# Attention in a graph network: both heads of a pair turned in one run of five pieces, two pairs behind the scores

## The chip, the core and the metric

The kernel runs on one core of a Trainium2 chip. The metric is device time in microseconds (us) from start to end of one launch, the median of several runs. Engines: TensorE (PE, with weight loads as PEld), VectorE (DVE), ScalarE (ACT), GpSimd (POOL) and the sync engine (SP), which issues DMAs.

## What is computed

A graph network over 1250 nodes with 512 features: a two-layer graph attention block, then a transformer block of two layers. The change touches only the attention of the transformer's layers, which is this part of the reference (cut):

```python
for l in range(L):                                   # L = 2, H = 8 heads of DH = 64
    q = ((x @ Wq[l].T + bq[l]) * scaling).reshape(n, H, DH)
    k = (x @ Wk[l].T).reshape(n, H, DH)
    v = (x @ Wv[l].T).reshape(n, H, DH)
    scores = jnp.einsum('ehd,ehd->eh', q[tgt], k[srcidx])
    m = jax.ops.segment_max(scores, tgt, num_segments=n)
    p = jnp.exp(scores - m[tgt])
    s = jax.ops.segment_sum(p, tgt, num_segments=n)
    w = p / (s[tgt] + 1e-16)
    agg = jax.ops.segment_sum(w[:, :, None] * v[srcidx], tgt, num_segments=n)
    attn = agg.reshape(n, D) @ Wo[l].T + bo[l]
    ...
```

The kernel does it densely: each score row of 1250 gets the logarithm of the edge count added (a large negative number where there is no edge), so a plain softmax over all nodes is the softmax over the edges.

## The kernel before

Nodes come in T = 10 tiles of P = 125 rows, heads in pairs (head 2c and 2c + 1 share 128 partitions of q and k). A unit u is one head of one tile of target nodes; a pair p is units 2p and 2p + 1; there are 80 units and 40 pairs in each of the two layers. `attend_parts` writes one program for each engine, all unrolled, and they meet in semaphores only.

**PE** (line 2017): for each p it makes the scores of pair p into banks 0 to 4 of PSUM (`score`, L1982, 18 matmuls of three precision passes), transposes the ten blocks of the even unit of pair p - 1 (`turn`, L2000), multiplies the turned probabilities of pair p - 2 with v (`weigh`, L2009, 40 matmuls, two heads side by side), and transposes the ten blocks of the odd unit of pair p - 1. A unit's transposes come in three pieces of 4, 3 and 3 blocks (`CUTS`). The pieces and the result of `weigh` (`out_bank`) take turns in banks 5, 6 and 7 (`ring`), seven tenants per pair. A piece may be written when the bank's former tenant is copied out.

**VectorE** (line 2106): for each p `mask` of both units (L2087: scores plus logs, and the row's maximum, in one instruction out of PSUM), now and then `lower_w` (L2104: low halves of a weight of the next stage), then for each of the two units `safe` (L2092), the reciprocal (L2096) and `divide` (L2098), which follow the unit's exponential.

**ScalarE** (line 2059): copies of the turned pieces to `probs_t` (`save_turned`, L2042), the exponential of the even unit (L2034), the copy of the result of pair p - 2 (`save_att`, L2049), the exponential of the odd unit, the copies of the odd unit's pieces, now and then `cut_w` (L2057).

`probs` has four slots, one per unit, `probs_t` four. The next score may start when both masks of the pair before are done, since it writes the same banks (`pe.wait_ge(masked, 2 * p)`). The weighing waits for the copies of its own pair and for the first copy of the run that precedes it, which empties its bank. The sync engine loads log tiles and weights in step with `masked` and `scored`. Before `attend` each layer projects q, k and v; after it comes a stage of its own (`stage_tail`).

Of the kernel before, what the change touches and what calls it, by code (L numbers as in the profile page):

```python
# [16 lines left out]
BANK = 512  # L17
# [1404 lines left out]
class LayerBuffers:  # L1422


    def __init__(self, k, ctx, gat, base, hidden):
# [21 lines left out]
        self.probs = self.wq  # L1447
        self.in_high = base
        ctx.enter_context(nc.sbuf_tensor("layer_room", [128, (self.e + 8 * D - base) // 4], F32))

# [397 lines left out]
def attend_parts(k, ctx, places, q_chunks, k_high, k_low, v_rows, logs, log_rows, weights, sources, att, x_rows, ln_b, x_biased):  # L1848
# [13 lines left out]
    TENANTS = 2 * PIECES + 1  # L1862
    biased = k.layer == 0
# [7 lines left out]
    probs_t = at("probs_t", [P, TURNED, T, P], F32, places.probs + 4 * SLOTS * N)  # L1871
    neg_max, sums, sums_safe, inverse = (sb(what, [P, COLUMNS]) for what in ("neg_max", "sums", "sums_safe", "inverse"))
# [7 lines left out]
    for rows, high, low in weights:  # L1880
# [4 lines left out]
    cut_at.update({(CHUNKS - 1) * PER_CHUNK + 3 + i: len(cuts) - late + i for i in range(late)})  # L1885
    shared_done, scored, masked, exp_done, sum_safe, inverted, divided, piece_turned, piece_saved, summed, att_saved = (
        k.sem(f"{what}_att{k.layer}") for what in ("shared_done", "scored", "masked", "exp_done", "sum_safe", "inverted", "divided",
                                          "piece_turned", "piece_saved", "summed", "att_saved"))

# [9 lines left out]

    def ring(pair, tenant):  # L1900
        return (5 + (pair * TENANTS + tenant) % 3) * BANK

    def turned(u, j):
        lo, hi = CUTS[j]
        at = ring(u // 2, j if u % 2 == 0 else PIECES + 1 + j)
        return k.psum[0:P, at:at + (hi - lo) * P]

    def out_bank(p):
        at = ring(p + 1, PIECES)
        return k.psum[:, at:at + P]  # L1910

# [3 lines left out]
    def own(odd):  # L1915
        return slice(odd * CH, (odd + 1) * CH)

    def column(u):
        return slice(u % COLUMNS, u % COLUMNS + 1)

    def attend_sync(sp):
# [42 lines left out]
    def attend_tensor(pe, by_rows):  # L1964
# [22 lines left out]

        def turn(u):
            q, odd = u // 2, u % 2
            pe.wait_ge(divided, u + 1)  # L1990
            for j, (lo, hi) in enumerate(CUTS):
                if odd and j == PIECES - 1:
                    if q >= 1:
                        pe.wait_ge(att_saved, q)
                elif odd:
                    pe.wait_ge(piece_saved, 2 * q * PIECES + j + 2)
                elif q >= 1:
                    pe.wait_ge(piece_saved, (2 * q - 1) * PIECES + j + 1)
                for i in range(lo, hi):
                    block_t = pe.transpose(turned(u, j)[:, (i - lo) * P:(i - lo + 1) * P],  # L2000
                                           probs[:, u % SLOTS, i * P:(i + 1) * P], k.ident[0:P, 0:P])
                block_t.then_inc(piece_turned, 1)

        def weigh(p):
            pe.wait_ge(piece_saved, (2 * p + 2) * PIECES + (1 if p + 1 < PAIRS else 0))
            for i in range(T):
                for u in (2 * p, 2 * p + 1):
                    odd, h = u % 2, u % H
                    total = pe.matmul(out_bank(p)[own(odd)], v_rows[:, i, h * CH:(h + 1) * CH],  # L2009
                                      probs_t[:, u % TURNED, i], start=i == 0, stop=i == T - 1)  # L2010
            total.then_inc(summed, 1)
# [4 lines left out]
        pe.wait_ge(k.q_low_done, CHUNKS)  # L2016
        for p in range(PAIRS + 2):
            if p < PAIRS:
                score(p)
            if p == 0:  # L2020
                by_rows(CHUNKS - 1, (1,))
            if p == 1:
                pe.wait_ge(k.v_saved, CHUNKS + 1)
            if 1 <= p <= PAIRS:
                turn(2 * p - 2)
            if p >= 2:
                weigh(p - 2)
            if 1 <= p <= PAIRS:
                turn(2 * p - 1)

    def attend_scalar(act, save_last_v):
        def exponential(u):
            act.wait_ge(masked, u + 1)
            act.activation(probs[:, u % SLOTS], probs[:, u % SLOTS], ACT.Exp, scale=-1.0,  # L2034
                           bias=neg_max[:, column(u)], accum_out=sums[:, column(u)]).then_inc(exp_done, 1)

        def save_turned(u):
            if u >= TURNED:
                act.wait_ge(summed, (u - TURNED) // 2 + 1)
            for j, (lo, hi) in enumerate(CUTS):  # L2040
                act.wait_ge(piece_turned, u * PIECES + j + 1)
                act.copy(probs_t[:, u % TURNED, lo:hi].rearrange("p c n -> p (c n)"), turned(u, j)).then_inc(piece_saved, 1)  # L2042

        def save_att(p):
            t = tile_of(2 * p)
            if p == 0:
                act.wait_ge(k.cols_stored, 16)
            act.wait_ge(summed, p + 1)
            act.copy(att[:, p % PER_TILE, t * P:(t + 1) * P], out_bank(p)).then_inc(att_saved, 1)  # L2049
# [9 lines left out]
        for p in range(PAIRS + 2):  # L2059
            if 1 <= p <= PAIRS:  # L2060
                save_turned(2 * p - 2)
# [6 lines left out]
            if p >= 2:  # L2068
                save_att(p - 2)
            if p < PAIRS:  # L2070
                exponential(2 * p + 1)
            if 1 <= p <= PAIRS:
                save_turned(2 * p - 1)
            if p in cut_at:
                cut_w(cut_at[p])

    def attend_vector(dve):
        def mask(u):
# [6 lines left out]
            if u >= SLOTS:  # L2085
                dve.wait_ge(piece_turned, (u - SLOTS + 1) * PIECES)
# [3 lines left out]
        def safe(u):  # L2090
            dve.wait_ge(exp_done, u + 1)
            dve.tensor_scalar(sums_safe[:, column(u)], sums[:, column(u)], TINY, None, ALU.add).then_inc(sum_safe, 1)  # L2092

        def divide(u):
            dve.wait_ge(sum_safe, u + 1)
            dve.reciprocal(inverse[:, column(u)], sums_safe[:, column(u)]).then_inc(inverted, 1)  # L2096
            dve.wait_ge(inverted, u + 1)
            dve.tensor_scalar(probs[:, u % SLOTS], probs[:, u % SLOTS], inverse[:, column(u)], None, ALU.mult  # L2098
                              ).then_inc(divided, 1)
# [5 lines left out]

        for p in range(PAIRS):
            mask(2 * p)
            mask(2 * p + 1)
# [677 lines left out]
```

## Time and profile before

| | us |
|---|---|
| median of 3 runs | 1716.58 (1715.73 to 1717.91) |
| the profiled execution | 1712.33 |
| its span | 1710.5 |
| PE busy in the span | 1554.0 (91%) |
| VectorE busy | 1293.1 (76%) |
| ScalarE busy | 1168.1 (68%) |

The mean granted clock of PE is 0.965 of full speed. The attention of layer 0 lies from about 876 to 1160 us of the span, that of layer 1 from about 1317 to 1601. The chain of work that ended last covers only the final stage, so it says nothing of these stretches; they are read from windows and from the timeline of a pair. A "releaser" is what ended an engine's idle time before an instruction.

### The profile page before, as it was taken

The numbers are of one execution on the slowest core, as the hardware profiler recorded it, in microseconds if no ns is written. First come the engines' busy times: TensorE is split into PE (matmuls) and PEld (weight loads), VectorE is DVE, ScalarE is ACT, GpSimd is POOL, SyncE is SP. The second block draws the span as 40 slices with busy tenths as digits, with TensorE's granted clock in tenths as the row PEclk, the third lists the DMA queues.
The fourth block names the chain that finished last, engine by engine and source line by source line (L and its number), as shares of the span: only waits on it lengthen the run. The fifth ranks groups of instructions, "written<-read, shape, count | busy, mean of one in ns | idle before, by whom it ended". The sixth has DMA issues, their size and how long they took to land. (4 is left out here: it accounts for less than half of the span.)

```text
span 1710.5 us, 35777 instructions
## 1 busy us (share of the span) xinstructions
PE 1554.0 (91%) x14602; PEld 1418.9 (83%) x14602; DVE 1293.1 (76%) x2259; ACT 1168.1 (68%) x2171; POOL 54.5 (3%) x67
## 2 busy tenths in 40 slices
PE   6899899999995888798999999998799999999882
PEld 3787899999975777787988888888798889889882
DVE  6995999989468999995347777776722777777577
ACT  3454788888655999896457788783433878888434
POOL 0000000000000100000000000001100000000030
PEclk9999899999997999899999999999899999999995
DMA  5113222300006321112412211104110021000401
GB/s 183 55 54 99 84 71 89 111 31 2 1 1 177 120 93 62 61 32 75 123 63 62 60 53 29 35 5 135 49 72 1 19 65 30 17 14 2 116 13 60
DMA packets 58517, 103.53 MB, mean 61 GB/s; under 512 B 15569, under 2 KB 33713, under 8 KB 58352
## 3 DMA queue, kind: packets, MB, share of 16 engines
q1 hardware_dynamic: 58352, 101.22, 19.0%
q8 instruction: 117, 1.92, 0.5%
q14 instruction: 48, 0.39, 0.1%
HBM read 75.74 MB, written 19.21 MB: 56 GB/s over the span
## 5 line engine op out<-in xcount | busy, mean ns | idle before, releaser
L2042 ACT COPY probs_t_att<-banks 125x375 f32<-125x375 f32 (+1 forms) x480 | 211.1, 515 | 73.9 <-PE banks L2000 73.6
L1028 PE MATMUL banks<-ident,probs_gat 125*125 125x125 f32 x1600 | 213.7, 283 | 45.8 <-ACT probs_gat L1132 44.9
L2087 DVE CUSTOM_DVE_ANT_0 probs_att<-banks,logs_or_y 125x1250 f32<-125x1250 f32 x160 | 227.1, 1457 | 28.8 <-PE banks L1982 28.8
L1028 PEld LDWEIGHTS banks<-ident,probs_gat 125*125 125x125 f32 x1600 | 194.5, 195 | 56.3 <-ACT probs_gat L1132 56.0
L1132 ACT ACTIVATE probs_gat<-probs_gat,neg_max_gat 125x1250 f32<-125x1250 f32 x160 | 214.8, 1342 | 33.3 <-DVE neg_max_gat L1301 33.0
L1301 DVE CUSTOM_DVE_ANT_0 probs_gat<-probs_gat,log_counts 125x1250 f32<-125x1250 f32 x160 | 235.3, 1471 | 0.1
L2034 ACT ACTIVATE probs_att<-probs_att,neg_max_att 125x1250 f32<-125x1250 f32 x160 | 216.0, 1350 | 10.0 <-DVE neg_max_att L2087 9.8
L2000 PE MATMUL banks<-ident,probs_att 125*125 125x125 f32 x1600 | 216.5, 282 | 2.9 <-ACT probs_t_att L2042 2.9
L2000 PEld LDWEIGHTS banks<-ident,probs_att 125*125 125x125 f32 x1600 | 186.5, 188 | 30.2 <-issue 16.1
L2009 PE MATMUL banks<-probs_t_att,v_rows 125*64 125x125 f32 x3200 | 189.5, 272 | 6.9 <-ACT probs_t_att L2042 2.0
L2009 PEld LDWEIGHTS banks<-probs_t_att,v_rows 125*64 125x64 f32 x3200 | 170.6, 136 | 22.0 <-ACT probs_t_att L2042 22.0
L1039 PE MATMUL banks<-h,probs_t_gat 125*125 125x128 f32 x1600 | 188.0, 273 | 0.0
L1039 PEld LDWEIGHTS banks<-h,probs_t_gat 125*125 125x125 f32 x1600 | 181.1, 188 | 0.0
L1982 PE MATMUL banks<-k_high,q_chunk 64*125 64x226 f32 (+2 forms) x960 | 158.8, 366 | 4.5 <-DVE q_chunk L1764 2.6
L2098 DVE TENSOR_SCALAR probs_att<-probs_att,inverse_att 125x1250 f32<-125x1250 f32 x160 | 139.5, 872 | 5.6
L1143 ACT COPY probs_t_gat<-banks 125x1250 f32<-125x1250 f32 x120 | 142.9, 1191 | 1.0 <-PE banks L1028 0.7
L1982 PEld LDWEIGHTS banks<-k_high,q_chunk 64*125 64x125 f32 x960 | 126.0, 183 | 15.4 <-issue 3.4
L1295 DVE SCALAR_TENSOR_TENSOR probs_gat<-a_pair,a_dst_gap 125x1250 f32<-125x1250 f32 x80 | 121.1, 1515 | 20.6 <-PE banks L1028 11.0
L1982 PE MATMUL banks<-k_low,q_chunk 64*125 64x512 f32 (+1 forms) x480 | 131.0, 350 | 0.0
L1295 DVE SCALAR_TENSOR_TENSOR probs_gat<-a_pair,a_dst_gap_gat 125x1250 f32<-125x1250 f32 x80 | 121.4, 1519 | 8.9 <-DMA a_pair<-a_src_rows 5.2
L2092 DVE TENSOR_SCALAR sums_safe_att<-sums_att 125x1 f32<-125x1 f32 x160 | 24.5, 153 | 85.8 <-ACT probs_att L2034 84.8
L547 PEld LDWEIGHTS banks<-offset_hot,key_hot_fr 125*125 125x125 bf16 x650 | 73.2, 139 | 16.5 <-DVE offset_hot L361 6.7
(258 smaller groups left out, 2932.4 us busy)
## 6 DMA issues: line engine op xcount, KB each, us to landing
a_pair<-a_src_rows SPq DMA_DIRECT2D x46, 625.0 KB, 4.9
logs_or_y<-log_rows SPq DMA_DIRECT2D x20, 546.9 KB
w_rows<-in_L_gnn_W_dram SPq DMA_DIRECT2D x12, 512.0 KB, 6.5
log_counts<-counts_fr SPq DMA_DIRECT2D x50, 122.1 KB
x_cols<-feature_cols SPq DMA_DIRECT2D x2, 2500.0 KB
logs_or_y<-x_cols SPq DMA_DIRECT2D x10, 500.0 KB, 5.2
x_rows_sb<-in_x_dram SPq DMA_DIRECT2D x1, 2240.0 KB
x_rows<-x_rows_sb SPq DMA_DIRECT2D x10, 224.0 KB
```

The lines of the kernel that those rows point to most:

```text
L1028: block_t = pe.transpose(turned(u)[:, i // 2, (i % 2) * P:(i % 2 + 1) * P], probs[:, u % PROBS, i * P:(i + 1) * P], k.ident[0:P, 0:P])
L1039: total = pe.matmul(out_bank(u), probs_t_slot(u)[:, i], rows, start=i == 0, stop=i == T - 1)
L1132: act.activation(probs[:, u % PROBS], probs[:, u % PROBS], ACT.Exp, scale=-1.0, bias=neg_max[:, column(u)], accum_out=sums[:, column(u)]). ...
L1143: act.copy(probs_t_slot(u).rearrange("p (b c) n -> p b (c n)", c=2), turned(u)).then_inc(probs_saved, 1)
L1295: dve.scalar_tensor_tensor(probs[:, u % PROBS], gat.pair[0:P, head % 2, 0], (gat.gap1, gap2)[layer][:, t, head:head + 1], gat.pair[0:P, he ...
L1301: dve.tensor_tensor_reduce(probs[:, u % PROBS], probs[:, u % PROBS], k.log_counts[:, t], -1.0, -FLOOR, ALU.add, ALU.min, neg_max[:, column ...
L1982: total = pe.matmul(k.psum[0:P, a:b], halves[own(o), half], keys[own(o), c, a - o * N:b - o * N], start=i == 0, stop=i == 2)
L2000: block_t = pe.transpose(turned(u, j)[:, (i - lo) * P:(i - lo + 1) * P], probs[:, u % SLOTS, i * P:(i + 1) * P], k.ident[0:P, 0:P])
L2009: total = pe.matmul(out_bank(p)[own(odd)], v_rows[:, i, h * CH:(h + 1) * CH], probs_t[:, u % TURNED, i], start=i == 0, stop=i == T - 1)
L2034: act.activation(probs[:, u % SLOTS], probs[:, u % SLOTS], ACT.Exp, scale=-1.0, bias=neg_max[:, column(u)], accum_out=sums[:, column(u)]). ...
L2042: act.copy(probs_t[:, u % TURNED, lo:hi].rearrange("p c n -> p (c n)"), turned(u, j)).then_inc(piece_saved, 1)
L2087: dve.tensor_tensor_reduce(probs[:, u % SLOTS], scores(u % 2), logs[:, t % KEPT], -1.0, -FLOOR, ALU.add, ALU.min, neg_max[:, column(u)]).t ...
```

## The change

PE now goes `score(p)`, then all twenty transposes of pair p - 2 in one run (`turn(p - 2)`), then `weigh(p - 3)`. The twenty blocks are five pieces of four, which take banks 5, 6, 7, 5, 6; the result of `weigh` always takes bank 7. So piece 3 waits for the copy of piece 0 and piece 4 for that of piece 1, in the same run; piece 1 of the next pair waits for the copy of piece 4, piece 2 for the copy of the result. `weigh` waits for the first three copies of the run before it.

ScalarE copies four pieces of each pair, then does both exponentials, then the copy of the result. VectorE copies the fifth piece (`save_last`), after the masks; its sum correction and reciprocal do both heads in one instruction each, and they and the divisions belong to pair p - 1. There are six slots of `probs` instead of four, and `probs_t` starts behind them. The room of the layer's buffers grows to hold it. The program is built with a scratch of 4096 bytes for software DMA.

```diff
-    SLOTS = 4
-    TURNED = 4
-    CUTS = ((0, 4), (4, 7), (7, 10))
-    PIECES = len(CUTS)
+    SLOTS, TURNED = places.SLOTS, places.TURNED
+    STEP = 4
+    PIECES = 2 * T // STEP
+    SAVED = PIECES - 1
...
+    def turned(j):
+        at = (5 + j % 3) * BANK
+        return k.psum[0:P, at:at + STEP * P]
...
+    def out_bank():
+        return k.psum[:, 7 * BANK:7 * BANK + P]
...
+        def turn(p):
+            pe.wait_ge(divided, 2 * p + 1)
+            for j in range(PIECES):
+                if j == 0 and p >= 1:
+                    pe.wait_ge(piece_saved, SAVED * p)
+                if j == 1 and p >= 1:
+                    pe.wait_ge(last_saved, p)
+                if j == 2 and p >= 2:
+                    pe.wait_ge(att_saved, p - 1)
+                if j >= 3:
+                    pe.wait_ge(piece_saved, SAVED * p + j - 2)
+                for n in range(j * STEP, (j + 1) * STEP):
+                    u, i = 2 * p + n // T, n % T
+                    if n == T:
+                        pe.wait_ge(divided, 2 * p + 2)
...
         def weigh(p):
-            pe.wait_ge(piece_saved, (2 * p + 2) * PIECES + (1 if p + 1 < PAIRS else 0))
+            pe.wait_ge(piece_saved, SAVED * (p + 1) + (3 if p + 1 < PAIRS else 0))
+            pe.wait_ge(last_saved, p + 1)
+            if p + 1 == PAIRS:
+                pe.wait_ge(att_saved, p)
...
-        for p in range(PAIRS + 2):
+        for p in range(PAIRS + 3):
             if p < PAIRS:
                 score(p)
...
-            if 1 <= p <= PAIRS:
-                turn(2 * p - 2)
-            if p >= 2:
-                weigh(p - 2)
-            if 1 <= p <= PAIRS:
-                turn(2 * p - 1)
+            if 2 <= p < PAIRS + 2:
+                turn(p - 2)
+            if p >= 3:
+                weigh(p - 3)
...
+        for p in range(PAIRS + 3):
             if p == 0:
                 save_last_v(0)
+            if 2 <= p < PAIRS + 2:
+                save_turned(p - 2)
             if p < PAIRS:
                 exponential(2 * p)
...
             if p < PAIRS:
                 exponential(2 * p + 1)
-            if 1 <= p <= PAIRS:
-                save_turned(2 * p - 1)
+            if p >= 3:
+                save_att(p - 3)
...
+        def save_last(p):
+            if p >= TURNED // 2:
+                dve.wait_ge(summed, p - TURNED // 2 + 1)
+            dve.wait_ge(piece_turned, (p + 1) * PIECES)
+            dve.tensor_copy(turned_to(p, SAVED), turned(SAVED)).then_inc(last_saved, 1)
...
+        for p in range(PAIRS + 2):
+            if p < PAIRS:
+                mask(2 * p)
+                mask(2 * p + 1)
+            if p >= 2:
+                save_last(p - 2)
             if p - 1 in cut_at:
                 lower_w(cut_at[p - 1])
-            for u in (2 * p, 2 * p + 1):
-                safe(u)
-                divide(u)
+            if 1 <= p <= PAIRS:
+                safe(p - 1)
+                invert(p - 1)
+                divide(2 * p - 2)
+                divide(2 * p - 1)
...
-    nc = bacc.Bacc("TRN2", target_bir_lowering=False, num_devices=1)
+    nc = bacc.Bacc("TRN2", target_bir_lowering=False, num_devices=1, dynamic_dma_scratch_size=4096)
```

## Rows read from the trace of the kernel before

Rows of a timeline are: start us, us, engine, line, operation, out<-in, shapes, count; in brackets the idle time before and its releaser.

**Rows 1.** Windows: stretch, us, busy of PE, PEld, DVE, ACT, POOL; clock, DMA.

```profile
876.00:1143.00 267.00, 262.78 (x2952) 237.34 (x2953) 206.77 (x396) 212.75 (x426) 14.37 (x17) 1.00 0.14 40
...
1317.00:1584.00 267.00, 262.87 (x2954) 237.33 (x2952) 206.56 (x395) 213.03 (x426) 0.00 (x0) 1.00 0.08 24
```

**Rows 2.** Timeline of a late pair of layer 1, PE: start, us, line.

```profile
1577.14 0.50 PE L1982 MATMUL banks<-k_high,q_chunk 64*125 64x226 f32 x2
...
1579.05 1.35 PE L2000 MATMUL banks<-ident,probs_att 125*125 125x125 f32 x10
...
1580.47 2.37 PE L2009 MATMUL banks<-probs_t_att,v_rows 125*64 125x125 f32 x40
...
1582.77 1.35 PE L2000 MATMUL banks<-ident,probs_att 125*125 125x125 f32 x10
...
1584.05 0.49 PE L1982 MATMUL banks<-k_high,q_chunk 64*125 64x226 f32 x2
```

**Rows 3.** Line 2000 (min/median/max ns), then weight loads of that pair.

```profile
L2000 PE MATMUL banks<-ident,probs_att x1600: 272/273/373, 883.3 to 1596.8; 125*125 125x125 f32 x178
...
1579.05 1.17 PEld L2000 LDWEIGHTS banks<-ident,probs_att 125*125 125x125 f32 x10 [0.16 <-DVE probs_att L2098]
...
1580.47 2.13 PEld L2009 LDWEIGHTS banks<-probs_t_att,v_rows 125*64 125x64 f32 x40 [0.26 <-ACT probs_t_att L2042]
```

**Rows 4.** Timeline of that pair, ScalarE; then groups (mean ns).

```profile
1579.84 0.58 ACT L2042 COPY probs_t_att<-banks 125x500 f32<-125x500 f32 x1 [1.07 <-PE banks L2000]
...
1579.84 0.95 ACT L2042 COPY probs_t_att<-banks 125x500 f32<-125x500 f32 x2 [1.07 <-PE banks L2000]
...
L2042 ACT COPY probs_t_att<-banks 125x375 f32<-125x375 f32 x160 | 68.4, 486 | 0.0
...
L2034 ACT ACTIVATE probs_att<-probs_att,neg_max_att 125x1250 f32<-125x1250 f32 x80 | 108.0, 1350 | 5.0 <-DVE neg_max_att L2087 4.9
```

**Rows 5.** The same pair, VectorE; then two groups that bear on the new copy.

```profile
1579.16 1.46 DVE L2087 CUSTOM_DVE_ANT_0 probs_att<-banks,logs_or_y 125x1250 f32<-125x1250 f32 x1 [0.31 <-PE banks L1982]
...
1581.92 0.08 DVE L2087 DVE_READ_ACCUMULATOR2_ANT neg_max_att<- 125x1 f32 x1
...
1582.53 0.15 DVE L2092 TENSOR_SCALAR sums_safe_att<-sums_att 125x1 f32<-125x1 f32 x1 [0.52 <-ACT probs_att L2034]
...
1582.91 0.87 DVE L2098 TENSOR_SCALAR probs_att<-probs_att,inverse_att 125x1250 f32<-125x1250 f32 x1
...
L2104 DVE TENSOR_TENSOR wo_low<-wo_rows,wo_high 128x512 fp32r<-128x512 f32 x4 | 2.8, 688 | 0.0
...
L1759 DVE TENSOR_TENSOR k_low<-banks,k_high x10: 1189/1200/1201, 800.3 to 1308.3; 128x1000 fp32r<-128x1000 f32 x10
```

**Rows 6.** Timeline at the start of layer 1: scores and first mask.

```profile
1316.82 0.50 PE L1982 MATMUL banks<-k_high,q_chunk 64*125 64x226 f32 x2 [1.29 <-DVE q_chunk L1764]
...
1318.96 1.46 DVE L2087 CUSTOM_DVE_ANT_0 probs_att<-banks,logs_or_y 125x1250 f32<-125x1250 f32 x1 [2.29 <-PE banks L1982]
...
1321.86 0.50 PE L1982 MATMUL banks<-k_high,q_chunk 64*125 64x226 f32 x2
...
1341.70 0.49 PE L1982 MATMUL banks<-k_high,q_chunk 64*125 64x226 f32 x2
```

**Rows 7.** Timeline where layer 1's attention ends.

```profile
1593.40 2.37 PE L2009 MATMUL banks<-probs_t_att,v_rows 125*64 125x125 f32 x40
...
1595.81 0.26 ACT L2049 COPY feature_cols<-banks 128x125 f32<-128x125 f32 x1 [1.72 <-PE banks L2009]
...
1600.28 0.26 ACT L2049 COPY feature_cols<-banks 128x125 f32<-128x125 f32 x1 [2.47 <-PE banks L2009]
```

**Rows 8.** Windows around a fall of the clock, and in layer 1's start.

```profile
1219.00:1226.00 7.00, 4.15 (x34) 3.81 (x33) 6.96 (x22) 0.00 (x0) 0.00 (x0) 1.00 0.00 0
...
1226.00:1236.00 10.00, 3.03 (x14) 3.03 (x15) 6.02 (x16) 8.17 (x14) 0.00 (x0) 0.50 0.38 98
...
1321.00:1328.00 7.00, 5.55 (x44) 4.53 (x44) 6.04 (x13) 5.62 (x11) 0.00 (x0) 1.00 0.00 0
```

More of the change, by code:

```diff
@@ L1422 @@
 class LayerBuffers:
+    SLOTS, TURNED = 6, 4
     def __init__(self, k, ctx, gat, base, hidden):
@@ L1447, in __init__ @@
         self.probs = self.wq
+        self.probs_t = self.probs + (4 * self.SLOTS * N + 31) // 32 * 32
         self.in_high = base
-        ctx.enter_context(nc.sbuf_tensor("layer_room", [128, (self.e + 8 * D - base) // 4], F32))
+        end = max(self.e + 8 * D, self.probs_t + 4 * self.TURNED * N)
+        ctx.enter_context(nc.sbuf_tensor("layer_room", [128, (end - base) // 4], F32))
     def at(self, name, shape, dt, place):
@@ L1870, in attend_parts @@
     probs = at("probs", [P, SLOTS, N], F32, places.probs)
-    probs_t = at("probs_t", [P, TURNED, T, P], F32, places.probs + 4 * SLOTS * N)
+    probs_t = at("probs_t", [P, TURNED, T, P], F32, places.probs_t)
     neg_max, sums, sums_safe, inverse = (sb(what, [P, COLUMNS]) for what in ("neg_max", "sums", "sums_safe", "inverse"))
@@ L1885, in attend_parts @@
     cut_at.update({(CHUNKS - 1) * PER_CHUNK + 3 + i: len(cuts) - late + i for i in range(late)})
-    shared_done, scored, masked, exp_done, sum_safe, inverted, divided, piece_turned, piece_saved, summed, att_saved = (
+    shared_done, scored, masked, exp_done, sum_safe, inverted, divided, piece_turned, piece_saved, last_saved, summed, att_saved = (
         k.sem(f"{what}_att{k.layer}") for what in ("shared_done", "scored", "masked", "exp_done", "sum_safe", "inverted", "divided",
-                                          "piece_turned", "piece_saved", "summed", "att_saved"))
+                                          "piece_turned", "piece_saved", "last_saved", "summed", "att_saved"))
     def scores(odd):
@@ L1898, in columns, with turned_to @@
         return found[-1:] + found[:-1] if odd == 0 else found[1:] + found[:1]
[L1900 to L1910, printed above, removed]
+    def turned(j):
+        at = (5 + j % 3) * BANK
+        return k.psum[0:P, at:at + STEP * P]
+    def turned_to(p, j):
+        rows = probs_t[:].rearrange("p (pair odd) c n -> p pair (odd c n)", odd=2)[:, p % (TURNED // 2)]
+        return rows[:, j * STEP * P:(j + 1) * STEP * P]
+    def out_bank():
+        return k.psum[:, 7 * BANK:7 * BANK + P]
     def tile_of(u):
@@ L1919, in column, with columns_of @@
         return slice(u % COLUMNS, u % COLUMNS + 1)
+    def columns_of(p):
+        return slice(2 * p % COLUMNS, 2 * p % COLUMNS + 2)
     def attend_sync(sp):
@@ L1986, in score @@
             total.then_inc(scored, 1)
[L1988 to L2000, printed above, removed]
+        def turn(p):
[13 more added lines that the diff above has]
+                        pe.wait_ge(divided, 2 * p + 2)
+                    block_t = pe.transpose(turned(j)[:, (n - j * STEP) * P:(n - j * STEP + 1) * P],
                                            probs[:, u % SLOTS, i * P:(i + 1) * P], k.ident[0:P, 0:P])
@@ L2008, in weigh @@
                     odd, h = u % 2, u % H
-                    total = pe.matmul(out_bank(p)[own(odd)], v_rows[:, i, h * CH:(h + 1) * CH],
+                    total = pe.matmul(out_bank()[own(odd)], v_rows[:, i, h * CH:(h + 1) * CH],
                                       probs_t[:, u % TURNED, i], start=i == 0, stop=i == T - 1)
@@ L2035, in exponential, with save_turned @@
                            bias=neg_max[:, column(u)], accum_out=sums[:, column(u)]).then_inc(exp_done, 1)
[L2037 to L2042, printed above, removed]
+        def save_turned(p):
+            if p >= TURNED // 2:
+                act.wait_ge(summed, p - TURNED // 2 + 1)
+            for j in range(SAVED):
+                act.wait_ge(piece_turned, p * PIECES + j + 1)
+                act.copy(turned_to(p, j), turned(j)).then_inc(piece_saved, 1)
         def save_att(p):
@@ L2048, in save_att @@
             act.wait_ge(summed, p + 1)
-            act.copy(att[:, p % PER_TILE, t * P:(t + 1) * P], out_bank(p)).then_inc(att_saved, 1)
+            act.copy(att[:, p % PER_TILE, t * P:(t + 1) * P], out_bank()).then_inc(att_saved, 1)
         def cut_w(i):
@@ L2057, in cut_w @@
             act.copy(high[:, a:b], rows[:, a:b]).then_inc(w_high_done, 1)
-        for p in range(PAIRS + 2):
-            if 1 <= p <= PAIRS:
-                save_turned(2 * p - 2)
+        for p in range(PAIRS + 3):
             if p == 0:
                 save_last_v(0)
+            if 2 <= p < PAIRS + 2:
+                save_turned(p - 2)
             if p < PAIRS:
@@ L2085, in mask, with safe, invert @@
             if u >= SLOTS:
-                dve.wait_ge(piece_turned, (u - SLOTS + 1) * PIECES)
+                dve.wait_ge(piece_turned, (u - SLOTS) // 2 * PIECES + PIECES)
             dve.tensor_tensor_reduce(probs[:, u % SLOTS], scores(u % 2), logs[:, t % KEPT],
                                      -1.0, -FLOOR, ALU.add, ALU.min, neg_max[:, column(u)]).then_inc(masked, 1)
-        def safe(u):
-            dve.wait_ge(exp_done, u + 1)
-            dve.tensor_scalar(sums_safe[:, column(u)], sums[:, column(u)], TINY, None, ALU.add).then_inc(sum_safe, 1)
+        def save_last(p):
+            if p >= TURNED // 2:
+                dve.wait_ge(summed, p - TURNED // 2 + 1)
+            dve.wait_ge(piece_turned, (p + 1) * PIECES)
+            dve.tensor_copy(turned_to(p, SAVED), turned(SAVED)).then_inc(last_saved, 1)
+        def safe(p):
+            dve.wait_ge(exp_done, 2 * p + 2)
+            dve.tensor_scalar(sums_safe[:, columns_of(p)], sums[:, columns_of(p)], TINY, None, ALU.add).then_inc(sum_safe, 1)
+        def invert(p):
+            dve.wait_ge(sum_safe, p + 1)
+            dve.reciprocal(inverse[:, columns_of(p)], sums_safe[:, columns_of(p)]).then_inc(inverted, 1)
         def divide(u):
-            dve.wait_ge(sum_safe, u + 1)
-            dve.reciprocal(inverse[:, column(u)], sums_safe[:, column(u)]).then_inc(inverted, 1)
-            dve.wait_ge(inverted, u + 1)
+            dve.wait_ge(inverted, u // 2 + 1)
             dve.tensor_scalar(probs[:, u % SLOTS], probs[:, u % SLOTS], inverse[:, column(u)], None, ALU.mult
@@ L2104, in lower_w @@
             dve.tensor_tensor(low[:, a:b], rows[:, a:b], high[:, a:b].bitcast(F32), ALU.subtract).then_inc(w_low_done, 1)
-        for p in range(PAIRS):
-            mask(2 * p)
-            mask(2 * p + 1)
+        for p in range(PAIRS + 2):
[4 more added lines that the diff above has]
+                save_last(p - 2)
             if p - 1 in cut_at:
                 lower_w(cut_at[p - 1])
-            for u in (2 * p, 2 * p + 1):
-                safe(u)
-                divide(u)
+            if 1 <= p <= PAIRS:
[3 more added lines that the diff above has]
+                divide(2 * p - 1)
     return attend_sync, attend_tensor, attend_scalar, attend_vector, attend_gpsimd
```

6 lines of the change are left out of this document (1 added, 5 removed).

## The prediction

> **What bounds the kernel now.** I read the windows first, because the change lies in the attention of two layers and the page's shares average over other stages. In each of the two stretches PE is busy for 263 of 267 us, with VectorE and ScalarE near 207 and 213 us, at a granted clock of 1.00 [rows 1]. PE is the bound, so what counts is the time between the start of one pair's scores and the next. The reader is to see in the timeline of one late pair where those 6.91 us go [rows 2]: scores 1.91 (1577.14 to 1579.05), ten transposes and what follows until the weighing starts 1.42 (to 1580.47), forty weighing matmuls 2.30 (to 1582.77), the other ten transposes 1.28 (to 1584.05). The same block of ten costs 1.42 before the weighing and 1.28 before the scores. The difference, 0.14, is a wait: the weight load of the weighing is released by ScalarE's copy [rows 3]. The rest is not waiting but starting: of the ten transposes nine last 273 ns and the first 373, they follow each other every 0.109 us ((1.35 - 0.27 - 0.10) / 9), and between the last start of a block and the first of the next lie 0.20 us (1.28 - 1.08). Each layer has 40 pairs; in layer 1 the first starts its scores at 1316.82 and the last at 1584.05 [rows 2, 6]. The windows of the two layers agree to 0.2 us, so I work one out and double it.
>
> **The change, PE in the steady state.** One run of twenty replaces two of ten. Two separate unwaited runs with their changeovers take 2 x 1.28 = 2.56 us; one takes 1.28 + 10 x 0.109 = 2.37. Together with the wait of 0.14, 0.33 us could go, and the period would be 1.91 + 2.37 + 2.30 = 6.58. But the run now holds two waits of its own, since five pieces pass through three banks: piece 3 needs the copy of piece 0, and piece 4 that of piece 1. ScalarE's first copy of a run starts 0.79 us after the first transpose (1579.84 against 1579.05), lasts 0.58, and PE moves 0.05 after its end (1580.47): a release at 1.42 [rows 2 to 4]. Piece 3 is the thirteenth transpose. The tenth weight load starts at 0.98 (1.17 less the 0.19 of a load), so the thirteenth would start at 0.98 + 3 x 0.109 = 1.31 [rows 3]. It is held by 0.11. The second copy starts 0.46 after the first (0.95 less 0.49 for a copy of 375 columns) and with 0.58 for 500 columns releases piece 4 at 0.79 + 0.46 + 0.58 + 0.05 = 1.88; its load, shifted, is due at 1.31 + 0.11 + 4 x 0.109 = 1.86 [rows 4]. That is 0.02 more. The weighing needs the third copy (bank 7 must be empty): 0.79 + 2 x 0.46 + 0.63 = 2.34, against a due time of 2.37 + 0.13 = 2.50, so it doesn't wait. I take a hold of 0.13 to 0.14 and a period of 6.72, 0.19 us less per pair. Ends: no hold gives 6.58. If copies went strictly one after another at 0.58, piece 4 would be released at 2.00, 0.25 late, and the weighing at 2.58, about on time: 6.83.
>
> A rule speaks against the joined run. The Trainium skill ("TensorE: Matmul & The Clock Gate", section The mechanism) says that a weight load overlaps a matmul in flight only when the row group differs; all transposes use the same 125 rows. By that rule there would be no overlap whose start-up a longer run saves, and the period would lose only the wait less the new hold, about nothing. The rows decide otherwise: with a spacing of 109 ns and loads of 0.19 us the loads do overlap here [rows 3].
>
> **VectorE and ScalarE in the steady state.** Per pair VectorE has two masks (1579.16 to 1582.00, 2.84 us), addition and reciprocal (1582.53 to 1582.91, 0.38; once for both heads instead of twice) and two divisions of 0.87 [rows 5]. The copy of 500 columns out of PSUM is new. No row shows it. The nearest that read PSUM are the 1000-column subtraction of 1.20 us and the mask of 1250 columns in 1.46; their slope of 1.04 ns gives 1.20 - 500 x 1.04 = 0.68. A division reads SBUF only and takes 0.87 for 1250, which would give 0.35. I take 0.69 (also the 512-column subtraction's 0.69) [rows 5]. Sum: 2.84 + 0.69 + 0.38 + 1.74 = 5.65, with a weight cut of 0.69 in eight of 40 pairs 6.34. Both are below 6.72. As to order: the masks end 4.87 us after the score start (1582.00 less 1577.14), the last transpose ends at 1.91 + 2.50 = 4.41 and a little, so the copy finds its piece ready; behind it on VectorE are the divisions, done at 7.7 (8.4 with a cut), needed by the run at 6.72 + 1.91 = 8.63 of the next iteration. The next mask is due at 6.72 + 2.02 = 8.74. ScalarE: four copies from 2.70 to about 4.7, two exponentials of about 1.35, one after the other, to 7.4, the copy of the result 0.26 [rows 7], a cut of about the same 0.69: done by 8.4 at the latest, and its next copy is due at 6.72 + 2.70 = 9.42 [rows 4]. Before, VectorE waited 0.52 us for an exponential in each pair [rows 5]; with the lag that wait goes, and it is covered by slack both ways, so I cost it at nothing. On the sync queue nothing is moved but the loads' waits come true earlier, and ten tiles of logs have many pairs of lead.
>
> **Filling and draining.** With times from the first score start: first mask 2.14, second score 5.04 as before [rows 6]. VectorE then goes straight to the third mask (score start + 2.02 = 7.06) instead of dividing, and the third score starts at 7.06 + 2.84 + 0.05 = 9.95. After the divisions (9.95 + 0.38 + 1.74 = 12.1) come the masks of the third pair, and the fourth score starts at 12.1 + 2.84 + 0.05 = 15.0; the second run of twenty and the first weighing fill PE to the fifth score at 15.0 + 6.72 = 21.8. Before it was 1341.70 - 1316.82 = 24.9 [rows 6]. The gain is 3.1. The 35 periods to the last score start give 35 x 0.19 = 6.7 more, together 9.8. Draining costs some of it back. Before, 16.5 us passed from the last score start to the end of the last copy (1584.05 to 1600.54) [rows 2, 7]. Now the run of pair 38 (of 0 to 39) starts after the next-to-last weighing, at 6.9 (its division is done at 4.87 + 0.69 + 0.38 + 0.87 = 6.8); weighing of 37 at 6.9 + 2.5 = 9.4; run of 39 at 9.4 + 2.3 = 11.7; weighing of 38 at 14.2; then bank 7 must be saved before the last weighing: 14.2 + 2.41 (1593.40 to 1595.81) + 0.26 + 0.05 = 16.9; and 2.41 + 0.26 more, 19.6. So 3.1 us more. Per layer 9.8 - 3.1 = 6.7 us, for two layers 13.4.
>
> The other edits (six probability slots, a larger room, a smaller scratch for software DMA, which these rows don't show in use) have no instruction on the path, 0 to 0.5 us either way.
>
> **Sum.** The profiled execution took 1712.33 us (span 1710.5); less 13.4 it gives 1698.9. The median of the runs is 1716.58, 4.2 above it for reasons outside the trace, so the forecast is 1716.58 - 13.4 = 1703.2. Without any hold the gain is 3.1 + 35 x 0.33 - 3.0 = 11.6 per layer, 1693.4. With the strict copies it is 3.1 + 35 x 0.08 - 3.2 = 2.7, 1711.2.
>
> **Rivals.** *Hold larger than its gain* (no or little change): the waits inside the run eat 0.25 or more, or VectorE's copy in the drain and the one bank 7 cost more. For it: the hold rests on margins of 0.02 to 0.15 us. Against: copies overlap by 0.12 us in the rows [rows 4]. Time 1711 to 1718.
>
> *The clock falls* (slower). In this trace it falls where PE worked with gaps: after 4.15 busy of 7 us it was granted 0.50 (1.2 instead of 2.4 GHz) for 10 us [rows 8]. The change makes one gap longer: between the second score (done at 5.04 + 1.91 = 6.95) and the third (9.95), 3.0 us in which PE has nothing, where before the first transposes stood. A fall loses half its length in PE-bound work, so 10 us low in each layer cost 10 us, and from 13.4 us low per layer on the change is slower; twice 20 us would give 1703.2 + 20 = 1723. Against it: the fill before had gaps as well (PE busy 5.55 of 7 us) and kept 1.00 [rows 8]. The Trainium skill ("TensorE: Matmul & The Clock Gate", section A second HAM failure mode: psum-queue depth-cycling) describes a clock that drops and recovers when PE idles briefly between groups while cycling PSUM banks. Neither stretch of rows 1 agrees with it, and the hold inside the run is smaller than the wait it replaces.
>
> *It doesn't do what it says*: no hold at all, because the first copy starts sooner than 0.79; then 1693.
>
> **Chances.** A measurement of this kernel can tell about 0.2%, 3.4 us, from no change. Forecast with a hold of 0.05 to 0.2 us: 0.58 (1697 to 1708). No hold: 0.14 (1691 to 1697). Large hold: 0.16 (1708 to 1718), half of it within 0.2%. Clock or another bound: 0.12, mostly above 1720. The range runs from 1691 to 1713. Faster 0.82, same 0.08, slower 0.10.
>
> **What would show it.** Score starts 6.7 us apart; twenty transposes whose last starts near 2.3 after the first, with about 0.1 idle at the thirteenth put down to ScalarE's copy, and no idle before the weighing; a VectorE copy of 500 columns near 0.69; fifth score 21.8 after the first; 19.6 from the last score to the last copy; clock 1.00. It is wrong if VectorE or ScalarE is found late at a run's start, if PE idles before scores in the steady state, or if the granted clock drops within the two stretches.

## The result and the profile after

The changed kernel took 1703.35 us, the median of 4 runs (1699.59 to 1707.93), against 1716.41 us before (1715.73 to 1717.91): a ratio of 0.9928 with a 95% interval of 0.9915 to 0.9941. The forecast was 1703.2. The profiled execution took 1707.93 us with a span of 1706.1. It is the slowest of the four, and its span is only 4.4 us below the span before. That is the first thing to clear up.

Windows of the changed kernel: the attention of layer 0 up to the last score, the stages between the two attentions, the attention of layer 1 (columns as in rows 1).

```profile
879.00:1138.00 259.00, 255.75 (x2897) 236.27 (x2899) 210.61 (x354) 187.34 (x347) 12.41 (x17) 0.99 0.15 41
...
1158.00:1318.00 160.00, 145.01 (x1070) 139.20 (x1071) 78.36 (x159) 58.66 (x99) 13.52 (x16) 0.93 0.23 68
...
1318.00:1577.00 259.00, 255.37 (x2894) 235.91 (x2894) 208.81 (x353) 186.89 (x347) 0.00 (x0) 0.99 0.08 24
```

And the stages between the two attentions in the kernel before, which the change doesn't touch:

```profile
1160.00:1317.00 157.00, 139.97 (x1071) 133.72 (x1073) 77.91 (x159) 58.93 (x99) 13.50 (x16) 0.97 0.23 70
```

The two attentions are shorter. From the first score to the last copy of the result they take 278.17 and 278.80 us where they took 283.46 and 283.73, so 10.2 us less. The stages between them do the same work in 160.6 us instead of 157.0, at a granted clock of 0.93 instead of 0.97; the stages ahead took 879.2 instead of 876.4, the last one 109.4 instead of 110.0. Together that is 5.8 us more in code that is the same, and 10.2 - 5.8 is the 4.4 of the span. The experiments below ask whether that belongs to the change.

The late pair of layer 1 in the changed kernel, all engines, answers to rows 2, 4 and 5 (merged timeline: start, us, engine, line):

```profile
1570.38 0.50 PE L1986 MATMUL banks<-k_high,q_chunk 64*125 64x226 f32 x2
...
1572.29 2.60 PE L2007 MATMUL banks<-ident,probs_att 125*125 125x125 f32 x20
...
1573.08 2.01 ACT L2050 COPY probs_t_att<-banks 125x500 f32<-125x500 f32 x4 [1.93 <-PE banks L2007]
...
1574.82 2.37 PE L2019 MATMUL banks<-probs_t_att,v_rows 125*64 125x125 f32 x40
...
1574.95 1.37 ACT L2042 ACTIVATE probs_att<-probs_att,neg_max_att 125x1250 f32<-125x1250 f32 x1
...
1575.16 0.68 DVE L2100 COPY probs_t_att<-banks 125x500 f32<-125x500 f32 x1
...
1576.15 1.65 DVE L2112 TENSOR_SCALAR probs_att<-probs_att,inverse_att 125x1250 f32<-125x1250 f32 x2
...
1577.12 0.50 PE L1986 MATMUL banks<-k_high,q_chunk 64*125 64x226 f32 x2
```

The period is 6.74 us (1570.38 to 1577.12) instead of 6.91. The scores and the changeover still take 1.91, the weighing with its changeover 2.30. What was 1.42 + 1.28 around the weighing is one run of 2.53 (1572.29 to 1574.82). Twenty transposes lie in a row of 2.60 us; at the spacing of rows 3 they would take 0.10 + 19 x 0.109 + 0.27 = 2.44. The missing 0.16 is the hold. ScalarE's first copy starts 0.79 after the run, as in rows 2 and 4.

The weight loads' waits in layer 1 (who waited for whom: us in total, times, longest), first before, then after:

```profile
PEld banks L2009 <- ACT probs_t_att L2042: 9.6, 37, 0.5
...
PEld banks L2000 <- DVE probs_att L2098: 6.9, 37, 0.6
```

```profile
PEld banks L2007 <- issue: 6.2, 36, 0.2
...
PEld banks L2007 <- ACT probs_t_att L2050: 0.3, 1, 0.3
```

The wait of the weighing for ScalarE, 9.6 us in 37 pairs, is gone. But the hold inside the run hardly shows among the waits: one of 0.3 us, where 37 runs were held. A matmul row of 273 ns outlasts the spacing of 109 ns, and a weight load's row of 189 ns does too, so a pause of 0.12 us between starts leaves next to no idle time. It is seen in the length of the group of twenty, and in the starts of the single weight loads in the trace. In the median of all 80 runs these are 0.109 us apart, but the thirteenth starts 0.224 after the twelfth and the seventeenth 0.156 after the sixteenth. That is 0.12 for piece 3 and 0.05 for piece 4.

The drain of layer 1, which answers to rows 7:

```profile
1583.86 2.60 PE L2007 MATMUL banks<-ident,probs_att 125*125 125x125 f32 x20
...
1588.69 2.60 PE L2007 MATMUL banks<-ident,probs_att 125*125 125x125 f32 x20
...
1593.63 0.26 ACT L2057 COPY feature_cols<-banks 128x125 f32<-128x125 f32 x1 [2.14 <-PE banks L2019]
...
1594.04 2.37 PE L2019 MATMUL banks<-probs_t_att,v_rows 125*64 125x125 f32 x40 [0.45 <-ACT feature_cols L2057]
...
1596.45 0.26 ACT L2057 COPY feature_cols<-banks 128x125 f32<-128x125 f32 x1 [2.55 <-PE banks L2019]
```

From the last score (1577.12) to the end of the last copy (1596.45 + 0.26) it takes 19.59 us.

### The profile page after: what moved, and what is told of

It reads as the page before. It is cut to its first block and busy times, and to the rows that moved or that the text cites. A ratio compares the mean times of both kernels' runs of the same rounds, so it can differ in the third digit from the quotient of the medians.

```text
span 1706.1 us, 35533 instructions
## 1 busy us (share of the span) xinstructions
PE 1555.9 (91%) x14602; PEld 1433.5 (84%) x14602; DVE 1305.3 (77%) x2179; ACT 1115.4 (65%) x2011; POOL 51.7 (3%) x67
## 5 line engine op out<-in xcount | busy, mean ns | idle before, releaser
L2050 ACT COPY probs_t_att<-banks 125x500 f32<-125x500 f32 x320 | 161.2, 590 | 137.8 <-PE banks L2007 137.8
L2007 PE MATMUL banks<-ident,probs_att 125*125 125x125 f32 x1600 | 209.0, 286 | 0.2
L2007 PEld LDWEIGHTS banks<-ident,probs_att 125*125 125x125 f32 x1600 | 191.1, 189 | 17.1 <-issue 13.3
L2112 DVE TENSOR_SCALAR probs_att<-probs_att,inverse_att 125x1250 f32<-125x1250 f32 x160 | 133.0, 874 | 2.8
L547 PE MATMUL banks<-offset_hot,key_hot_fr 125*125 125x250 bf16 x650 | 81.6, 281 | 7.2 <-issue 7.1
```

The lines of the kernel that those rows point to most:

```text
L547: product = pe.matmul(sums(g), key_hot[:, g % 2, r, 0:P], offset_hot[:, (first[g] + r) % RING], start=r == 0, stop=r == R - 1)
L2007: block_t = pe.transpose(turned(j)[:, (n - j * STEP) * P:(n - j * STEP + 1) * P], probs[:, u % SLOTS, i * P:(i + 1) * P], k.ident[0:P, 0:P])
L2050: act.copy(turned_to(p, j), turned(j)).then_inc(piece_saved, 1)
```

## The experiments

All ran against the kernel before on the same chip. The edits of "The lag and the slots without the joined run" and of "The smaller scratch alone" were made to the kernel before, the others to the changed kernel; where an edit is long, only its main lines are shown. "Period" is the median distance of score starts in the profiled execution, from the sixth pair on.

### The changed kernel again

> The changed kernel, unchanged, a second look. In its profiled execution (1707.9 us) attention took 278.2 and 278.8 us per layer instead of 283.5 and 283.7, 10.2 us less, but the other stages took 5.8 us more, with more stretches at the granted clock of 0.5. Theory: the period of 6.74 us and the drain of 19.6 us come back to 0.02 us in every execution, and the times of the runs differ (1699.6 to 1707.9) only by where the clock falls. Expected 1703 us +- 4, attention 277 to 279 us per layer, and with fewer low stretches in the other stages a span below 1706. Rival: the change itself slows the other stages (the larger room, the smaller scratch); then the stages before 879 us and between the layers are again 3 us longer at the same clock record.

> The changed kernel once more, beside the next run on the same chip. Expected 1703 us +- 1.5; attention 277.1 us per layer where the clock doesn't fall in the fill, 278 to 279 where it does.

Measured: 1703.12 us (1700.54 to 1706.95), ratio 0.9927 (0.9900 to 0.9954), and 1704.70 us (1696.21 to 1707.62), ratio 0.9932 (0.9913 to 0.9951). The periods are 6.74 and the drains 19.59 to 19.60 in both layers of both executions. The attentions took 277.07 and 278.81 us in one, 277.02 and 278.80 in the other. The stages ahead took 878.4 and 877.4, the stages between 159.0 both times, the last one 109.4. So the change is steady in its own stretches. The rest scatters, and it does so in code that is the same in all twelve traces. The stages ahead of the first attention took 875.2 to 876.5 us in the four traces with 61.4 us at a granted clock of 0.50 in that part, and 880.5 and 880.6 in the two with 71.7. The stages between took 157.0 to 157.1 us in the three traces with 10.2 us low, 160.6 in the one with 23.9. Kernels with the room and the scratch of the change are among the quick ones of both (876.0 and 157.1), so the 5.8 us aren't the change's own cost. Over the runs the changed kernel scatters more than the one before: 1696 to 1708 against 1712 to 1719.

### The lag and the slots without the joined run

```diff
-            if 1 <= p <= PAIRS:
-                turn(2 * p - 2)
-            if p >= 2:
-                weigh(p - 2)
-            if 1 <= p <= PAIRS:
-                turn(2 * p - 1)
+            if 2 <= p < PAIRS + 2:
+                turn(2 * p - 4)
+            if p >= 3:
+                weigh(p - 3)
+            if 2 <= p < PAIRS + 2:
+                turn(2 * p - 3)
```

> The lag of two and the six slots alone: as before, three pieces per head, ten transposes before and ten after the weighing, but of pair p - 2 and the weighing of p - 3; divisions one pair later; all copies on ScalarE. Theory (the joined run and the removed wait make the gain): the period stays 1.91 + 1.42 + 2.30 + 1.28 = 6.91 us, the fill gains about 3 us per layer and the drain gives about 3 back, so 1716 us, within 3 us of before. Rival (the lag makes the gain, by taking exponentials and divisions out of a cycle): period 6.74 and about 1703 us.

Measured: 1720.01 us (10 runs), ratio 1.0021 (1.0008 to 1.0033), period 6.915 and 6.917. Its PE timeline late in layer 1:

```profile
1500.51 0.49 PE L1984 MATMUL banks<-k_high,q_chunk 64*125 64x226 f32 x2
...
1502.41 1.35 PE L2002 MATMUL banks<-ident,probs_att 125*125 125x125 f32 x10
...
1503.83 2.37 PE L2011 MATMUL banks<-probs_t_att,v_rows 125*64 125x125 f32 x40
...
1506.12 1.35 PE L2002 MATMUL banks<-ident,probs_att 125*125 125x125 f32 x10
...
1507.41 0.49 PE L1984 MATMUL banks<-k_high,q_chunk 64*125 64x226 f32 x2
```

1.90, 1.42, 2.29, 1.29: the four parts of rows 2, unchanged, although the divisions are ready long before. The lag alone brings nothing in the steady state. The total is 4 us over the 1716 expected (and outside the 3 us allowed), and the step that was off is the drain: it takes 21.7 us instead of 16.5. One pair more has to go through two runs and a weighing without a score beside it, 5.2 us, where I had reckoned with about 3. The fill gains 3.1 at most, and here a fall of the clock took part of that in both layers (score distances of 6.06 and 6.35 where 4.9 was due).

### All five copies on ScalarE

```diff
                 act.copy(turned_to(p, j), turned(j)).then_inc(piece_saved, 1)
+            act.wait_ge(piece_turned, (p + 1) * PIECES)
+            act.copy(turned_to(p, SAVED), turned(SAVED)).then_inc(last_saved, 1)
...
-            if p >= 2:
-                save_last(p - 2)
```

> The changed kernel with the fifth piece copied by ScalarE too, after its other four, instead of by VectorE. Theory (PE is the bound, ScalarE idles about 1.9 us per pair before a run): the period stays 6.74 us to 0.02 and the time 1703 us within 3. Rival (VectorE's help carries the change): ScalarE is late for the next run by the 0.59 us of a copy, period 7.0 to 7.3, 1725 to 1750 us.

Measured: 1703.98 us, ratio 0.9937 (0.9915 to 0.9959), period 6.737 and 6.736. ScalarE late in layer 1:

```profile
1499.64 2.01 ACT L2050 COPY probs_t_att<-banks 125x500 f32<-125x500 f32 x4 [1.46 <-PE banks L2007]
...
1501.51 0.62 ACT L2052 COPY probs_t_att<-banks 125x500 f32<-125x500 f32 x1
...
1501.98 1.38 ACT L2042 ACTIVATE probs_att<-probs_att,neg_max_att 125x1250 f32<-125x1250 f32 x1
...
1503.31 1.37 ACT L2042 ACTIVATE probs_att<-probs_att,neg_max_att 125x1250 f32<-125x1250 f32 x1
...
1504.63 0.29 ACT L2059 COPY feature_cols<-banks 128x125 f32<-128x125 f32 x1
...
1506.38 2.01 ACT L2050 COPY probs_t_att<-banks 125x500 f32<-125x500 f32 x4 [1.46 <-PE banks L2007]
```

It does five copies, two exponentials and the result, and still waits 1.46 us for PE before the next run. VectorE's share in the copying is worth 0.36 us per layer, in the drain (19.95 instead of 19.59), and nothing in the steady state.

### Shorter copies of the first two pieces

```diff
-                act.copy(turned_to(p, j), turned(j)).then_inc(piece_saved, 1)
+                part = slice(0, (2 if j < 2 and p >= TURNED // 2 else STEP) * P)
+                act.copy(turned_to(p, j)[:, part], turned(j)[:, part]).then_inc(piece_saved, 1)
```

> The changed kernel, but the copies of pieces 0 and 1 take only 250 of their 500 columns from the third pair on (half of those probabilities are left out of the weighing, old ones stand in their place). Their banks are free about 0.25 us sooner. Theory (the run is held 0.16 us by the waits of pieces 3 and 4 for these copies): last transpose 2.17 us after the first instead of 2.33, period 6.59, 0.15 x 37 pairs x 2 layers = 11 us less than the changed kernel, about 1692 us. Rival (twenty in a row are slower for another reason, or the weighing takes the wait over): the period stays within 0.03 of 6.74.

Measured: 1691.52 us, ratio 0.9862 (0.9841 to 0.9883), period 6.587 and 6.590. PE late in layer 1:

```profile
1500.74 2.45 PE L2007 MATMUL banks<-ident,probs_att 125*125 125x125 f32 x20
...
1503.12 2.37 PE L2019 MATMUL banks<-probs_t_att,v_rows 125*64 125x125 f32 x40
...
1507.34 2.44 PE L2007 MATMUL banks<-ident,probs_att 125*125 125x125 f32 x20
```

This kernel leaves half of the columns of two pieces out of the weighing and so computes something else; only its times are of use. The group of twenty is 2.44 to 2.45 us long, as the spacing demands, and the weighing follows 2.38 after the run's start instead of 2.53. The thirteenth and the seventeenth weight load now start 0.109 us after their forerunners like the rest. The hold is these copies, and it is 0.15 us per pair.

### A first copy that takes twice as long

```diff
+                if j == 0:
+                    act.copy(turned_to(p, j), turned(j)).then_inc(copied, 1)
+                    act.wait_ge(copied, p + 1)
                 act.copy(turned_to(p, j), turned(j)).then_inc(piece_saved, 1)
```

> The changed kernel, but ScalarE copies the first piece of each run twice, one copy after the other. The release of that bank comes about 0.65 us later, and the second, third and fourth copies with it. Theory (the hold answers to these copies one for one): held by 0.65 more, period 7.35 to 7.4, total 0.64 x 77 = 49 us more than the changed kernel, about 1752 us. Rival (the copy's end isn't what the run waits for): less than 0.2 us per pair.

Measured: 1752.23 us (2 runs), ratio 1.0213 (1.0186 to 1.0241), period 7.350 and 7.345. PE late in layer 1:

```profile
1506.81 1.57 PE L2009 MATMUL banks<-ident,probs_att 125*125 125x125 f32 x12
...
1508.83 1.18 PE L2009 MATMUL banks<-ident,probs_att 125*125 125x125 f32 x8 [0.45 <-ACT probs_t_att L2055]
...
1509.94 2.37 PE L2021 MATMUL banks<-probs_t_att,v_rows 125*64 125x125 f32 x40
...
1514.14 1.57 PE L2009 MATMUL banks<-ident,probs_att 125*125 125x125 f32 x12
```

Now that the pause is long enough the profile shows it: twelve transposes, 0.45 us idle put down to ScalarE, eight more. 7.35 less 6.74 is 0.61 for a copy that was sized at 0.65.

### The joined run with the old lags and slots

```diff
-            if 2 <= p < PAIRS + 2:
-                turn(p - 2)
-            if p >= 3:
-                weigh(p - 3)
+            if 1 <= p <= PAIRS:
+                turn(p - 1)
+            if p >= 2:
+                weigh(p - 2)
...
+            if p < PAIRS:
+                divide(2 * p)
+                divide(2 * p + 1)
```

> The joined run of five pieces and the single result bank, but with the lags and the four slots of before: score(p), turn(p - 1), weigh(p - 2), divisions in the same turn of VectorE's loop after each head's exponential. Theory (the run is the gain, the second lag only lengthens the drain): the divisions are ready 1.0 and 0.8 us before the run needs them (7.65 and 8.9 us after the score start, needed at 8.65 and 9.75), so the period is 6.74 as with the lag of two; the fifth score starts about 24.5 us after the first instead of 21.8, the drain takes about 16 instead of 19.6. Per layer 24.5 + 35 x 6.74 + 16 = 276.4 us, 1 to 2.4 less than the changed kernel: about 1700 us. Rival (the lag of two is needed): the first exponential waits for the four copies, the division is late, and the period is 6.85 to 7.2, 1707 to 1730 us.

> The joined run with the lags and slots of before, beside the changed kernel on the same chip. Attention took 276.0 us per layer in its first look, against 277.1 to 278.8. Theory: 2 to 4 us below the changed kernel, 1700.5 us +- 1.5, with intervals against before that hardly meet. Rival: the two are the same within 1 us, the difference of the first looks being where the clock fell in other stages.

Measured: 1700.81 us (1700.18 to 1702.11), ratio 0.9912 (0.9896 to 0.9929), and 1702.96 us (1701.30 to 1704.25), ratio 0.9922 (0.9909 to 0.9935). The periods lie between 6.739 and 6.748, the fifth score 24.4 after the first, the drain takes 15.47. Late in layer 1:

```profile
1501.73 2.60 PE L2007 MATMUL banks<-ident,probs_att 125*125 125x125 f32 x20
...
1504.26 2.37 PE L2019 MATMUL banks<-probs_t_att,v_rows 125*64 125x125 f32 x40
...
1505.89 0.15 DVE L2104 TENSOR_SCALAR sums_safe_att<-sums_att 125x1 f32<-125x1 f32 x1 [0.52 <-ACT probs_att L2042]
...
1507.21 0.15 DVE L2104 TENSOR_SCALAR sums_safe_att<-sums_att 125x1 f32<-125x1 f32 x1
...
1508.47 2.60 PE L2007 MATMUL banks<-ident,probs_att 125*125 125x125 f32 x20
```

VectorE waits 0.52 us for the exponential again, as in rows 5, and its division of the first head ends at 1507.15, 1.3 us ahead of the next run at 1508.47. So the second lag isn't needed for the joined run. Attention takes 276.0 to 276.1 us in all four stretches, against 277.0 to 278.8 with the lag of two. Measured beside each other on one chip, their medians are 1702.96 and 1704.70, and their intervals overlap widely: the 2 to 4 us that I expected are not there in the total. That this version beats the changed kernel is shown for the attention stretches; for the whole time 1 to 2 us are likely, but not shown. It beats the kernel before by 0.8 to 0.9%.

### The v matmuls divided over two gaps

```diff
-            if p == 0:
-                by_rows(CHUNKS - 1, (1,))
+            if p < 2:
+                by_rows(CHUNKS - 1, (1,), range(2 * p, 2 * p + 2))
```

> The changed kernel with the last twelve v matmuls cut in two: six after the first scores, six after the second, where PE has nothing to do for 3.0 us (ScalarE saves them one pair later). Theory (a fall of the clock in the fill comes from that gap and costs 0.9 to 1.5 us per layer where it comes): no low stretch within 20 us of the first score of a layer, score distances 5.04, 4.93, 4.93, 6.7 in both layers, 1 to 3 us less, about 1701 us. Rival (the fall has another cause, for it came in one of the two executions in layer 0 and in both in layer 1): the low stretches of 3.4 us stay, 1703 us.

Windows over the fill of layer 1, first the changed kernel, then this one:

```profile
1323.00:1327.60 4.60, 1.94 (x18) 1.68 (x18) 2.61 (x3) 2.93 (x4) 0.00 (x0) 1.00 0.01 2
...
1327.60:1331.00 3.40, 3.11 (x18) 3.11 (x18) 2.13 (x6) 1.70 (x4) 0.00 (x0) 0.50 0.00 0
```

```profile
1311.00:1316.00 5.00, 3.54 (x26) 2.75 (x26) 2.85 (x4) 1.44 (x3) 0.00 (x0) 1.00 0.02 3
...
1316.00:1321.00 5.00, 3.64 (x26) 2.83 (x26) 2.97 (x6) 2.87 (x5) 0.00 (x0) 1.00 0.00 2
...
1321.00:1326.00 5.00, 4.53 (x40) 4.18 (x42) 4.86 (x8) 4.19 (x8) 0.00 (x0) 1.00 0.00 0
```

Measured: 1701.15 us (1699.06 to 1702.04), ratio 0.9913 (0.9897 to 0.9930). In the changed kernel PE is busy for 1.94 of 4.6 us after the second score, and then the clock is granted at 0.50 (1.2 instead of 2.4 GHz) for 3.41 us. With six matmuls in each gap it is busy for 3.5 or 3.6 of every 5 us and keeps 1.00 in both layers. The score distances are 5.0, 4.94, 4.93 and 6.69 in both layers, and the attentions take 277.07 and 277.35 us. That is one trace with two fills, and the changed kernel's clock stayed up in two of its own six, so this trace alone doesn't settle it; the count over all kernels below does more. That this kernel's total is below the changed kernel's isn't shown, since the two were not measured side by side.

### The smaller scratch alone

```diff
-    nc = bacc.Bacc("TRN2", target_bir_lowering=False, num_devices=1)
+    nc = bacc.Bacc("TRN2", target_bir_lowering=False, num_devices=1, dynamic_dma_scratch_size=4096)
```

> The kernel before with the smaller scratch for software DMA only. Theory: nothing, 1716.5 us within 2, period 6.91, and the stages outside attention as in before (876 us ahead, 157 between, 110 behind). Rival: the smaller scratch is what shifts the low stretches of the other stages in the changed kernel (878 to 879 ahead, 159 to 161 between): then 1718 to 1722 us.

Measured: 1714.90 us (10 runs), ratio 0.9996 (0.9986 to 1.0005). Period 6.914, stages of 876.5, 157.0 and 110.0 us. It does nothing.

## Why the prediction was right

**The period.** Forecast 6.72, measured 6.74. Its terms: scores and changeover 1.91 (1.91), run to weighing 2.50 (2.53), weighing 2.30 (2.30). The hold was put at 0.13 to 0.14 and is 0.15, by the shortened copies. The weight loads show where the hold sits: 0.12 at the thirteenth (0.11 forecast) and 0.05 at the seventeenth (0.02 forecast). The joining itself can be read as the difference between two kernels with the same lag and all copies on ScalarE: 6.915 (two runs) against 6.737 (one run), 0.18 us per pair. The bound "no hold" was 6.58, and the kernel with short copies has 6.59. The other bound, strict copies, didn't come: four copies lie in 2.01 us, so they start 0.47 to 0.48 apart though each lasts 0.58.

**VectorE and ScalarE.** The new copy was put at 0.69 from the slope of two rows that read PSUM, and takes 0.67 in the mean. That VectorE's and ScalarE's new order costs nothing was right with room to spare, as the fifth copy on ScalarE shows.

**The fill.** Forecast 21.8 us to the fifth score. Where the clock stays up it is 21.6 (5.04, 4.93, 4.93, 6.69); in the profiled execution it was 22.7 and 23.0. The named gap of 3.0 us after the second score did bring a fall, the mechanism that I had given as the slower rival. It was mis-sized there, not misplaced: the prediction reckoned with 10 us low per layer, and one stretch of 3.41 us came. It makes the fill 1.1 to 1.5 us longer (22.7 to 23.1 instead of 21.6), since part of it lies in idle time, and it doesn't come back in the steady state. The traces with that gap show it in 9 of 14 fills, those without it (the kernel before twice, old lags twice, divided v once) in none of 10. The Trainium skill ("TensorE: Matmul & The Clock Gate", section A second HAM failure mode: psum-queue depth-cycling) describes a clock that oscillates because PE idles briefly and often between groups while the banks are cycled. The traces here don't show that: through the steady state, with banks cycled and short waits in every pair, the clock stayed at 1.00, and the fall came after a single gap of 3 us.

**The drain.** Forecast 19.6, measured 19.59.

**The sum.** 6.7 us per layer were forecast; an attention without a fall is 6.4 us shorter (283.46 less 277.07), with a fall 4.9 to 5.3. That makes 10 to 13 us for both layers, against a difference of the medians of 13.1 in the first measurement, 13.5 and 10.6 in the two later ones. The hit to 0.2 us is luck: the medians of the same kernel differ by 1.6 us, the fill gained 0.2 more per layer and the period 0.4 less than forecast, a fall of the clock in some of the fills was not in the sum, and in the profiled execution other stages gave back 5.8. The scratch is ruled out as a cause of that. Over the twelve traces the time of these stages goes with how long the clock was low in them. Ahead of attention that can't depend on when attention ends, so it differs from one execution to the next; whether the changed length of attention also moves the low stretches behind it is left open, since no run held everything else fixed.

**The rivals.** No hold, large hold and the lag as the cause are excluded by the shortened copies, by the periods and by the lag without the joined run. The rule against the joined run that the prediction takes from the Trainium skill ("TensorE: Matmul & The Clock Gate", section The mechanism: a weight load overlaps a running matmul only when the row group differs) would have left the period at about 6.9. The group of twenty in 2.44 us with the short copies shows the spacing of 109 ns kept over the whole run. Two signs came out otherwise. I expected an idle time of 0.1 at the thirteenth transpose put down to ScalarE; the start is late by that much, but no idle time is listed. And I had called the prediction wrong if the granted clock drops within the two stretches: it did, for 3.41 us in each layer of the profiled execution. By that sign the forecast of a clock of 1.00 was wrong; what saved the time is that the drop was a third of the 10 us reckoned with, and came once.

## What to carry over

When an engine is the bound and its work alternates between kinds, count the changeovers. Here each costs 0.19 us: the first start of the new kind comes 0.20 after the last of the old and the second 0.21 after the first, where work of one kind follows itself in 0.11. Merging two runs of ten saved one changeover per pair without removing any work. A longer run needs its buffers back sooner; check the reuse distance against the full way of a buffer (last write, start of the copy, its length, the wake-up: here 0.36 + 0.58 + 0.05 = 0.99 us against 0.87 us of work in two pieces). Look for the hold in the length of the group and in the single starts, since a pause shorter than one instruction's row leaves no idle time. A deeper lag is worth its longer drain only if something is in fact late: the same run with the old lags has the same period, a drain 4.1 us shorter and a fill only 2.8 us longer.

## What the runs showed of the hardware

After a pause of 3.0 us on PE (about 7.0 to 10.0 us after the first score) the granted clock fell 9.5 to 11.5 us after the first score and stayed low for 3.41 us, in 9 of 14 fills. With the pause cut in two, of 1.4 to 1.5 us each, it stayed up in both fills of the one trace, and in all 8 fills of the kernels that never had the pause. Between starts of fp32 transposes of 125x125 lie 0.109 us at the full clock, while a weight load's row lasts 0.189 and a matmul's 0.273, all on the same 125 rows of the array: in the trace they overlap. A run of transposes held for 0.12 us shows no idle time of PE. A copy of 125x500 out of PSUM takes 0.58 us on ScalarE and 0.67 on VectorE.
